# Gated cross-attention layer on one core: queries turned by a DMA transpose, layer 2's weight maxima before layer 1's

## The reference

```python
# mixer: 64 heads of width 8, sequence length 1024, batch 8
kv  = einsum('bhil,bhjl->bijhl', k, v)            # k = v = ctx
y   = causal convolution of kv with ssm_kernel[h] (by FFT of length 2048)
out = einsum('bijhl,bhil->bjhl', y + kv * D, q)   # q = layernorm(x)
x   = x + tanh(g_xattn) * out
# feed-forward: W1 (4096 x 1024), W2 (1024 x 4096)
def mx_quant(x):                                  # blocks of 32 along the last axis
    amax  = max(abs(block)); scale = exp2(floor(log2(amax)) - 6)
    return clip(round(block / scale), -128, 127) * scale
h = layernorm(bf16(layernorm(x))) * ln_w + ln_b
h = bf16(mx_quant(gelu(bf16(mx_quant(h) @ mx_quant(W1).T + b1))) @ mx_quant(W2).T + b2)
x = x + tanh(g_ffn) * bf16(residual + h)
```

## Time and profile before

| | us |
|---|---|
| runs (3) | 1983.58, 1983.67, 1988.19 |
| median | 1983.67 |
| the profiled execution's own time | 1986.38 |
| its span, first to last instruction | 1984.5 |
| PE busy | 1899.7 |
| DVE busy | 1694.7 |
| POOL busy | 956.1 |
| ACT busy | 755.0 |

### The profile page before, as it was taken

One profiled execution on the slowest core, in us unless ns is written; L12 is line 12 of the kernel. 1 busy time (PEld: TensorE's weight loads), 2 busy tenths in 40 slices (PEclk: granted clock), 3 DMA queues, 4 the chain that ended last, 5 costly groups with the idle time before them and its releaser, 6 DMA issues. The chain is left out here.

```text
span 1984.5 us, 29456 instructions
## 1 busy us (share of the span) xinstructions
PE 1899.7 (96%) x11632; PEld 1498.6 (76%) x11680; DVE 1694.7 (85%) x2082; ACT 755.0 (38%) x1036; POOL 956.1 (48%) x1028
## 2 busy tenths in 40 slices
PE   6999999999999999999966997999999999999998
PEld 5988888888888898888954764666777666666773
DVE  6899999998897889898879798998888888898843
ACT  4333333333333433333303641444455444444440
POOL 4888899888898999999950000000000000000000
PEclk9999999999999999999978998999999999999999
DMA  6544446566644554555448412212222111221112
GB/s 247 192 174 157 157 153 205 207 229 216 222 172 153 192 190 166 194 181 193 143 162 336 150 43 75 67 62 64 75 75 75 65 54 64 75 67 51 54 43 75
DMA packets 99274, 271.75 MB, mean 137 GB/s; under 512 B 41472, under 2 KB 41472, under 8 KB 90944
## 3 DMA queue, kind: packets, MB, share of 16 engines
q1 hardware_dynamic: 99136, 269.86, 39.8%
HBM read 218.91 MB, written 42.53 MB: 132 GB/s over the span
## 5 line engine op out<-in xcount | busy, mean ns | idle before, releaser
L318 PE MATMUL y_ps<-kk_hi,slab 128*128 128x352 f32 (+6 forms) x3328 | 896.2, 351 | 21.0 <-DMA slab<-taps_scratch 17.7
L318 PEld LDWEIGHTS y_ps<-kk_hi,slab 128*128 128x128 f32 x3328 | 595.5, 189 | 90.1 <-issue 21.8
L318 PE MATMUL y_ps<-kk_lo,slab 128*128 128x512 f32 (+6 forms) x1664 | 581.0, 349 | 0.0
L976 PE MATMUL acc_ps<-w_T,arena 128*128 128x512 bf16 x2000 | 439.5, 379 | 2.5
L961 PE MATMUL l_ps<-f_xq_T,w_T 128*128 128x256 bf16 x3584 | 397.8, 274 | 15.6 <-ACT arena L1022 10.9
L961 PEld LDWEIGHTS l_ps<-f_xq_T,w_T 128*128 128x128 bf16 x3584 | 352.4, 98 | 61.9 <-ACT arena L1022 11.5
L976 PEld LDWEIGHTS acc_ps<-w_T,arena 128*128 128x128 bf16 x2048 | 200.4, 98 | 238.4
L1271 POOL TENSOR_TENSOR f_rstd<-f_var_eps,f_neg_half 128x1 f32<-128x1 f32 x28 | 15.3, 547 | 698.3 <-DVE f_var_eps L1081 698.3
L318 PEld LDWEIGHTS y_ps<-kk_lo,slab 128*128 128x128 f32 x1664 | 314.4, 189 | 34.4
L1022 ACT ACTIVATE arena<-l_ps,f_b 128x256 bf16<-128x256 f32 x512 | 213.2, 473 | 252.5 <-PE l_ps L961 247.4
L509 DVE TENSOR_TENSOR upper<-y_ps,q_ext 128x768 f32<-128x768 f32 (+1 forms) x128 | 155.9, 1218 | 97.1 <-PE y_ps L318 91.5
(11 more groups left out here) (135 smaller groups left out, 2061.9 us busy)
## 6 DMA issues: line engine op xcount, KB each, us to landing
slab<-taps_scratch SPq DMA_DIRECT2D x128, 512.0 KB, 4.8
arena<-in_w_m SPq DMA_DIRECT2D x32, 1024.0 KB, 6.4
arena<-x_scratch SPq DMA_DIRECT2D x60, 512.0 KB, 3.8
k_ext<-in_ctx_e SPq DMA_DIRECT2D x64, 384.0 KB, 3.5
arena<-in_w SPq DMA_DIRECT2D x18, 1024.0 KB, 6.9
x_tile<-in_x_t SPq DMA_DIRECT2D x32, 512.0 KB, 6.2
out_t<-arena SPq DMA_DIRECT2D x32, 512.0 KB, 2.6
x_scratch<-x SPq DMA_DIRECT2D x31, 512.0 KB, 4.5
```

The lines of the kernel that those rows point to most:

```text
L318: mm = nc.tensor.matmul(y_ps[:, y_base + begin:y_base + end], slab[s][:, half, d * P:(d + 1) * P], kk_part[s][:, begin - d * PAIR:end - d ...
L976: mm = nc.tensor.matmul(acc_ps[s][:, c * 512:(c + 1) * 512], hidden[g % 2][:, k, s * P:(s + 1) * P], w2_T[:, k, c * 512:(c + 1) * 512], st ...
```

## The change

Queries. For tiles after the first, PE no longer turns xn. ACT copies xn, seen as 16-bit words, into `xn_halves`: all low halves, then all high halves (`split_halves`, 128 x 2048 words). SP turns that by one DMA transpose with 16-bit elements into `q_halves` (`turn_halves`). `take_q` joins the halves: four ACT copies that read a low and a high half in turn and write them side by side into q_ext. The two buffers lie in the tiles of the taps, which have served by then. Only the first tile is still turned by PE.

Weights. The maxima of layer 2 come first: heads 0 to 5, then 7, 9, ..., 25, through two buffers. Layer 2's scales stand at head 26, and its pieces are spread over heads 27 to 63 (37 heads; 29 before). Beside them stand the maxima of layer 1, at heads 27, 28, 30, 31, 33, 34, 36, 37, 39, 40, 42, 43, 45, 46, 48 and 49, whose loads all go through one buffer, `w1_raw`. Layer 1's inverses stand at head 50, the spreads at 52, 54, 56 and 58.

```diff
-    maxima_heads = list(range(6)) + list(range(7, early_heads + 5, 2))
-    maxima_heads += [early_heads + 5 + 2 * n // 3 for n in range(2 * W_TILES - len(maxima_heads))]
-    scales_head = maxima_heads[-1] + 1
-    maxima_slot = [n % 2 if n < 12 else (n - 12) % 3 for n in range(2 * W_TILES)]
-    spread_heads = [scales_head + 2 + scales_head % 2 + 2 * i for i in range(4)]
-    w2_heads = heads - scales_head - 1
+    maxima2_heads = list(range(6)) + list(range(7, early_heads + 11, 2))
+    scales2_head = maxima2_heads[-1] + 1
+    maxima1_heads = [scales2_head + 1 + 3 * n // 2 for n in range(W_TILES)]
+    scales1_head = maxima1_heads[-1] + 1
+    spread_heads = [scales1_head + 2 + scales1_head % 2 + 2 * i for i in range(4)]
+    w2_heads = heads - scales2_head - 1
...
+        xn_halves = taps_all[:, 0:L].bitcast(I16).rearrange("p (h l) -> p h l", h=2)
+        q_halves = taps_hi_all[:, 0:L].bitcast(I16).rearrange("p (n c) -> p n c", c=P)
-        w_raw = w2_raw = [raw_weights(arena, i) for i in (2, 3, 0)]
+        w2_raw, w1_raw = [raw_weights(arena, i) for i in (2, 3, 0)], raw_weights(arena, 1)
...
+            def load_maxima2(n):
+                if n >= 2:
+                    sp.wait_ge(max2_ready, n - 1)
+                sp.dma_start(w2_raw[n % 2], w_m[W_TILES + n]).then_inc(maxima2_loaded[n % 2], 16)
+
+            def load_maxima1(n):
+                if n == 0:
                     sp.wait_ge(e_input, EARLY)
+                    for turned in e_turned:
+                        sp.wait_ge(turned, 16 * EARLY // 2)
+                else:
+                    sp.wait_ge(max1_ready, n)
+                sp.dma_start(w1_raw, w_m[n]).then_inc(maxima1_loaded, 16)
...
+            def turn_halves(t):
+                sp.wait_ge(halves_ready, t)
+                if t >= 2:
+                    sp.wait_ge(q_ready, t)
+                sp.dma_start(q_halves, xn_halves.rearrange("p h l -> p (h l)"), transpose=True).then_inc(halves_turned, 16)
...
                     load_k(h + 3)
+                if h % TILE_HEADS == 1 and t + 1 < tiles:
+                    turn_halves(t + 1)
                 if h % TILE_HEADS == 1 and t >= 1:
                     store_x1(t - 1)
...
+                if h - 1 in maxima2_heads and maxima2_heads.index(h - 1) + 2 < W_TILES:
+                    load_maxima2(maxima2_heads.index(h - 1) + 2)
+                if h == scales2_head:
+                    load_maxima1(0)
                     for j in range(3):
                         load_w2(j)
+                if h - 1 in maxima1_heads and maxima1_heads.index(h - 1) + 1 < W_TILES:
+                    load_maxima1(maxima1_heads.index(h - 1) + 1)
...
                         turn_back(t - 1)
-                    if h % TILE_HEADS == 1 and i == 2 and t + 1 < tiles:
-                        turn_q(t + 1)
...
+            def split_halves(t):
+                act.wait_ge(xn_ready, t + 1)
+                if t == 1:
+                    act.wait_ge(taps_lo_ready, 1)
+                else:
+                    act.wait_ge(halves_turned, 16 * (t - 1))
+                nc.scalar.copy(xn_halves, xn[:].bitcast(I16).rearrange("p (l h) -> p h l", h=2)).then_inc(halves_ready, 1)
+
             def take_q(t):
-                act.wait_ge(q_turned, t + 1)
+                act.wait_ge(halves_turned, 16 * t)
                 if t >= 2:
                     act.wait_ge(products_ready, 2 * TILE_HEADS * (t - 1))
+                for part in range(TILE_HEADS):
+                    words = q_ext[t % 2][part][:].bitcast(I16).rearrange("p n (c h) -> p n c h", h=2)
+                    for first, count in ((0, CH), (CH, EXT - CH)):
+                        source = view(taps_hi_all.bitcast(I16), part * CH, [(P, LB), (1, count), (LB * P, 2)])
+                        done = nc.scalar.copy(words[:, :, first:first + count, :], source)
+                done.then_inc(q_ready, 1)
...
                     if h % TILE_HEADS == 0:
                         ln_apply(t + 1)
+                        split_halves(t + 1)
...
+            def layer1_maxima(n):
+                nb = HID // 2 // QB
+                dve.wait_ge(maxima1_loaded, 16 * (n + 1))
+                nc.vector.tensor_reduce(w_max[:, n * nb:(n + 1) * nb], w1_raw.rearrange("p (k i) -> p k i", k=nb),
+                                        AX.X, ALU.max, apply_absolute_value=True).then_inc(max1_ready, 1)
...
+                if h in maxima2_heads:
+                    layer2_maxima(maxima2_heads.index(h))
+                if h in maxima1_heads:
+                    layer1_maxima(maxima1_heads.index(h))
+                if h == scales2_head:
+                    layer2_scales()
+                if h == scales1_head:
+                    layer1_scales()
```

More of the change, by code:

```diff
@@ L162, in mixer_block @@
         k_loaded = [sem("k_loaded0"), sem("k_loaded1")]
-        w_loaded = [sem(f"w_m_loaded{i}") for i in range(3)]
-        w_max_ready, w_floor, w_bits, w_inv_ready = sem("w_max_ready"), sem("w_floor"), sem("w_bits"), sem("w_inv_ready")
+        maxima2_loaded, maxima1_loaded = [sem("w2_m_loaded0"), sem("w2_m_loaded1")], sem("w1_m_loaded")
+        max2_ready, max1_ready, w_floor, w_bits, inv2_ready, inv1_ready = (
+            sem(n) for n in ("w2_max_ready", "w1_max_ready", "w_floor", "w_bits", "w2_inv_ready", "w1_inv_ready"))
         w2_ints, w2_clipped, w2_quant = sem("w2_ints"), sem("w2_clipped"), sem("w2_quant")
@@ L442, in _ @@
             copy_k(1)
-            take_q(0)
+            take_first_q()
             for h in range(heads):
@@ L636, in layer2_quant, with weight_inverses, layer2_scales, layer1_scales @@
                                         w2_scale_twice, ALU.mult).then_inc(w2_quant, 1)
-            def weight_scales():
-                dve.wait_ge(w_max_ready, 2 * W_TILES)
-                nc.vector.tensor_scalar(w_max[:], w_max[:], TINY, None, ALU.max).then_inc(w_floor, 1)
-                dve.wait_ge(w_floor, 1)
-                upper_half = w_max[:].bitcast(U16).rearrange("p (n two) -> p n two", two=2)[:, :, 1]
-                nc.vector.tensor_scalar(w_inv.bitcast(U16), upper_half, EXP_BITS, EXP_BITS,
-                                        ALU.bitwise_and, ALU.bitwise_xor).then_inc(w_bits, 1)
-                dve.wait_ge(w_bits, 1)
-                nc.vector.tensor_scalar(w_inv, w_inv, float(QB), None, ALU.mult).then_inc(w_inv_ready, 1)
-                dve.wait_ge(w_inv_ready, 1)
+            def weight_inverses(layer, n):
+                maxima = w_max[:, layer * L:(layer + 1) * L]
+                inverse = w_inv[:, layer * L:(layer + 1) * L]
+                nc.vector.tensor_scalar(maxima, maxima, TINY, None, ALU.max).then_inc(w_floor, 1)
+                dve.wait_ge(w_floor, n)
+                upper_half = maxima.bitcast(U16).rearrange("p (n two) -> p n two", two=2)[:, :, 1]
+                nc.vector.tensor_scalar(inverse.bitcast(U16), upper_half, EXP_BITS, EXP_BITS,
+                                        ALU.bitwise_and, ALU.bitwise_xor).then_inc(w_bits, 1)
+                dve.wait_ge(w_bits, n)
+                return nc.vector.tensor_scalar(inverse, inverse, float(QB), None, ALU.mult)
+            def layer2_scales():
+                dve.wait_ge(max2_ready, W_TILES)
+                weight_inverses(1, 1).then_inc(inv2_ready, 1)
+                dve.wait_ge(inv2_ready, 1)
                 nc.vector.tensor_scalar(w2_scale.bitcast(U16), w_inv[:, L:2 * L].bitcast(U16), -1.0, 254.0 * 128,
-                                        ALU.mult, ALU.add).then_inc(w_inv_ready, 1)
+                                        ALU.mult, ALU.add).then_inc(inv2_ready, 1)
+            def layer1_scales():
+                dve.wait_ge(max1_ready, W_TILES)
+                weight_inverses(0, 2).then_inc(inv1_ready, 1)
             def residual(t):
```

90 lines of the change are left out of this document (36 added, 54 removed).

## The result

| | before | after |
|---|---|---|
| median of runs, us | 1985.35 | 2008.61 |
| lowest and highest | 1983.58, 1988.19 | 2006.12, 2010.69 |
| ratio, 95% interval | | 1.011 [1.0097, 1.0122] |
| own time of the profiled execution | 1986.38 | 2006.12 |
| its span | 1984.5 | 2004.3 |

The account below looks back on a forecast made before the run. PE was taken to set the pace, with DVE and POOL close behind. The span summed as 1984.5 - 27 + 5 + 37 - 1 = 1998.5 us; the forecast median was 1998 us, slower, range 1973 to 2020.

Parts of the forecast that it names:

- part 4: Layer-1 maxima, heads 27 to 49: single-buffer loads come late, DVE and then PE wait, clock slows; +37 us, bounds 19 and 55.
- the old wait in head 37: Head 37 before: PE's wait of 3.04 us plus slow clock (3.0 + 2.4), from ACT keeping inverses after its normalisation.
- Part 1: Query transposes leave PE: 31 sets of 0.87 us, -27.0 us if nothing else becomes late.
- Part 2: ACT's split 1.91 us, its take of q 7.2, transpose landing about 5.5; hidden in a relaxed head.
- Part 3: Heads 8 to 21: DVE is the bound and keeps the stretch at about 190 us; +5 us against the query gain.
- the 6 to 8 named as a sign: PE waits of 6 to 8 us after DVE's load waits in heads 31, 37, 43, 49, with clock near 0.5.
- the lesser waits: PE waits in heads 28, 29, 34, 41 and 51, from three pieces in one head; together 3.0 us.
- The lower bound of 19: Layer-1 maxima cost if the odd-head load lands at 16.1 us into the head, with no clock loss.
- (b): Rival, chance 0.14: transposes run beside everything, layer-1 maxima cost 19 + 3, or POOL can't follow; 1983 us, no change.
- Part 5: Spread inverses, heads 52 to 58: four PE waits of 1 us replace head 37's loss; -1 us, bounds -5 and +15.
- (a): Rival, chance 0.19: layer-1 loads arrive in time or DVE's lateness stays under 2; their cost is under 10, total 1970 us.
- (c): Rival, chance 0.11: ACT is the bound, transpose lands in 10.8 us, high half late, 1.5 us per pair; about 2020 us.

Follow-up runs that it names:

- away: e_keep with layer 2's maxima in heads 0 to 7 and 22 to 29, none in heads 8 to 21; 1971.05 us, 0.9913 of before.
- early: The changed kernel with the next layer-1 load asked for at the top of the head, right behind the slab; 1977.97 us, 0.995 of before.
- plain: The changed kernel with the query transposes replaced by plain copies of the same bytes, queries not transposed; 2003.05 us, 1.0076 of before.
- e_keep: The changed kernel with layer-1 loads at the top of the head and ScalarE keeping spread inverses before normalisation and split; 1969.77 us, 0.9911 of before.
- queries kernel: The kernel before with the query part of the change alone, weight tables, buffers and order as before; 1984.16 us, 0.9981 of before.
- q_low: The query part alone, with one of POOL's adds of each head made by VectorE from head 22 on; 1990.39 us, 1.0017 of before.
- best: e_keep with one of POOL's adds of each head made by VectorE from head 22 on; 1995.41 us, 1.0044 of before.
- mid: The changed kernel with the next layer-1 load asked for behind the k load, ahead of transpose, store and x load; 1987.46 us, 1.0 of before.

## Why the prediction was right, point by point

The span's 19.8 us by stretches, against the forecast's own terms:

| stretch | forecast | measured |
|---|---|---|
| to head 8: 4 query sets | -3.5 | -3.1 |
| 8-20: 6 sets -5.2, +5 for DVE | 0 | +0.7 |
| 20-28: 4 sets | -3.5 | -0.9 |
| 28-52: 12 sets -10.4, part 4 +37, the old wait in head 37 -5.4 | +21 | +19.9 |
| 52-61: 5 sets -4.4, four spread waits +4 | -0.4 | +1.1 |
| behind it | 0 | +2.1 |
| sum | +14 | +19.8 |

**Part 1, the query sets.** 0.87 us per set is right: quiet odd heads take 15.43 us, and four sets before head 8 give 3.5. What failed is the clause "if nothing else becomes late", beyond heads 8 to 21: with the queries alone the 27 us shrink to 3.8. Each stretch's excess over its own no-stall row, less that of before, shares it out: heads 9 to 28 keep 7.2 us (12.2 less 5.0), much of it DVE's load, since away takes 5.6 off; 28-52 keeps 7.9 (15.9 less 8.0), of which the wait for the spread's copy is 2.7 (8.7 less 6.0); 52-61 keeps 5.3, where DVE waits for POOL (each within 1 us, by PE's first matmuls). Some 3 to 5 us of the rest lie before head 1 and behind the mixer and vary as much between kernels that are alike there. In stretch 28-52 of the whole change this loss was hidden behind the waits for loads; early leaves 367.9 us where PE needs 360.

**Part 2, ScalarE and DMA.** The split took 1.90 us, as forecast. take_q was mis-sized, 7.2 us taken from the strided row: the rows of ACT from 50 to 1000 us are

```profile
L424 ACT COPY q_ext<-taps_hi 128x1024 int16<-128x1024 int16 x59 | 69.1, 1171 | 106.0 <-DMA taps_hi<-taps 106.0
L414 ACT COPY taps<-xn 128x2048 int16<-128x2048 int16 x30 | 57.0, 1901 | 1.0
L424 ACT COPY q_ext<-taps_hi 128x512 int16<-128x512 int16 x59 | 39.8, 675 | 0.0
```

and a tile's four copies take 3.40 us together, the dense bound. The rule of the Trainium skill ("SBUF — State Buffer", "Door 1: The DMA port swizzle") does not show here: each read is 2 KB from the last, at the dense price of 1171 ns for 1024 elements, while L444 takes 2345 for as many 32-bit words at a stride of 128 bytes. It cost nothing in the sum, since ScalarE had time either way (it waits 106 us for these transposes). The transpose: issue 3.19 us (median of 31; I took 2.5), landing 5.0 (5.5); plain has 0.47 and 4.2. In head 31, where the queue of transfers binds, this makes no difference, and over the whole kernel the plain copy gains about 6 us. By the Trainium skill ("Advanced Engine Details and Errata", "X-Bar Transpose (TRN2)") a transposing DMA is as fast as a plain one; here it is 0.8 us slower to land and holds SP 2.7 us longer.

**Part 3, heads 8 to 21.** Right on 8 to 20: 190.2 for a forecast 190, and away shows the reason. The stretch does not end there, though: heads 21 and 22 took 33.4 us (30.0 without stall), which I had not carried on.

**Part 4, the term that decides.** The late load, the heads and the size held: waits of DVE of 7.8, 7.4, 7.0 and 6.4 in heads 31, 37, 43 and 49, and early takes them away for 30 us. Head 31 by steps: load asked for at s + 13.8, forecast s + 10.4 + 3.8 = 14.2; landed at s + 21.8, forecast 22.4. Two errors offset each other here: DVE entered the head 2.6 us late, not 3.8, and the queue ahead of the load was 0.8 longer.

The forecast had the place of PE's wait wrong. It let PE wait for the low half, at the end of the head, once DVE is more than 3.7 us late. In heads 32, 38, 44 and 50 PE waits instead 8.3 us into the head, before its third stretch, for DVE's last product of the head before (`lower`, L544, in the rows above; the code waits there for `products_ready`). In head 32 that product ends 13.7 us in: 5.5 us, where the forecast had 8.1. The four waits are 5.5, 5.0, 5.3 and 3.2 us, 19 in all, not 28.5, and below the 6 to 8 named as a sign. The clock made up for it: the four heads were 8.3, 7.5, 7.8 and 5.0 us longer than 14.57, 28.5 in all, so 9.6 is work at the lower level (2.8, 2.5, 2.5 and 1.8), where I had 5, because I took part of it as hidden behind a wait at the head's end. In head 32 no such wait came. That 28.5 stands in both sums is luck; with the clock the forecast had 33.5.

And the lesser waits cost 9.8 us, not 3.0 (0.5 of it is the spread's own work in head 52): heads 35 and 36 together 1.9, and heads 51 and 52 together 5.0. Three pieces in one head with a maximum before them weigh more than I took. The lower bound of 19 for this part leaves out the 3 us of lesser waits that rival (b) adds.

**Part 5, the spread inverses.** Three waits show, 0.6, 0.4 and 2.3 us; forecast four of 1. The stretch 52-61 is 4.0 us above e_keep's 136.9, in which none is left, as the forecast's 4 has it. What the table's forecast left out is that the spreads' own 0.5 us per head moves with them: 1.5 us more here and as much less in 28-52. In early one of the waits is 4.5 us and the part costs 8.

**The rivals.** (a)'s condition, loads in time, was met only in early, whose 1978 is 8 above its 1970 (its own terms add up to 1971). (b)'s clause on POOL, "it is busy 366.5 of 375", was a real limit in heads 53 to 61 of the queries kernel, beneath the loads. (c) did not show: DVE's waits for the high half went from 5.9 to 8.4 us.

## What to carry to other kernels

Where one engine asks for all transfers in order, the cost of having a single buffer can lie in where its next request stands among waits and transfers: here moving two lines turned +1.1% into -0.5%, and two more made it -0.9%. Before counting work taken from the busiest engine as gain, ask for each stretch how far away the second and third engines are; of 27 us taken from PE, 3.8 arrived. And a cheap operation that another engine waits for goes ahead of long work that nobody wants yet.

## What the runs showed of the hardware that I had not expected

POOL's spans are not its work. The same add of 320 elements per partition takes 3.19 us in the queries kernel and 0.89 in q_low, means of ten from 830 to 985 us:

```profile
L782 POOL TENSOR_TENSOR upper<-upper,lsum 128x320 f32<-128x320 f32 x10 | 31.9, 3194 | 0.0
```

```profile
L791 POOL TENSOR_TENSOR upper<-upper,lsum 128x320 f32<-128x320 f32 x10 | 8.9, 892 | 0.0
```

In the queries kernel, head 55, it lies beside DVE's low half (888.77 to 892.03 us). POOL's rows around it:

```profile
888.73 0.89 POOL L780 TENSOR_TENSOR upper<-upper 128x320 f32<-128x320 f32 x1
889.57 3.19 POOL L782 TENSOR_TENSOR upper<-upper,lsum 128x320 f32<-128x320 f32 x1
892.71 0.89 POOL L784 TENSOR_TENSOR upper<-upper,lsum 128x120 f32<-128x120 f32 x1
```

In q_low, where the add is gone and the order shifts, the long one is an operation on one element per partition, in the same window:

```profile
L766 POOL TENSOR_TENSOR rstd<-var_eps,neg_half 128x1 f32<-128x1 f32 x5 | 14.3, 2863 | 0.0
```

Its mean is 0.55 us in the queries kernel. And DVE's low half varies with what lies beside it, from 2.7 us before to 2.9 in e_keep and 3.2 in best. That the two hold each other up is the reading that fits these rows; no run here had one of them alone.

The issue of a transposing DMA is no fixed price: 1.3 to 4.4 us in the changed kernel, 5.57 in mid, where it stands right behind a 1 MB load.
